# Metaformer layer on one core: the last unit of the scan at 384 tokens, its dense experts as one-hot column blocks, experts 0 and 1 finished in two pieces, four result buffers

## The reference, cut to what matters

```python
x = x + conv_ref(_ln_c(x), ...)          # Mamba block: in_proj, conv, selective scan, out_proj, norm, proj
t = _to_tokens(x)                        # 4 * 1024 tokens of 64 channels
t = t + ffn_ref(_ln_t(t), ...)           # 8 experts, one for each token, capacity 640

def step(h, inp):                        # the scan, over the 1024 tokens of an image, 128 channels, 16 states
    u_t, d_t, B_t, C_t = inp
    dA = jnp.exp(d_t[..., None] * A)
    h = dA * h + (d_t * u_t)[..., None] * B_t[:, None, :]
    y = jnp.einsum('bdn,bn->bd', h, C_t)

logits = x @ gate_w + gate_b             # ffn_ref
idx = jnp.argmax(softmax(logits)); prb = probs[idx]
pos = cumsum(one_hot)[idx] - 1           # rank of the token in its expert
kept = pos < C                           # C = 640
buf = zeros((E, C, D)).at[idx, pos_safe].set(x, mode='drop')
hmid = relu(einsum('ecd,edf->ecf', buf, w1) + b1)   # 64 -> 256
ybuf = einsum('ecf,efd->ecd', hmid, w2) + b2        # 256 -> 64
y_tok = ybuf[idx, pos] * (prb * kept)
```

## Time and profile before

| | us |
|---|---|
| median of 3 runs | 415.32 (412.15 to 419.61) |
| span of the profiled execution, first to last instruction | 398.3 |
| what lies around the span, if the profiled execution was a median one | 17.0 |
| busy: PE, DVE, ACT, POOL | 306.8, 308.8, 235.3, 281.8 |
| granted TensorE clock, mean | 0.880 of full speed |
| moved by DMA | 78.68 MB |

### The profile page before, as it was taken

The page is one execution under the profiler, slowest core; times in us unless marked ns, Lnnn a source line. Parts: engine busy times, 40 slices in busy tenths (PEclk is TensorE's granted clock), DMA queues, the critical chain, the costliest instruction groups (busy, mean ns, idle before and its releaser), DMA issues. The chain is left out here.

```text
span 398.3 us, 4350 instructions
## 1 busy us (share of the span) xinstructions
PE 306.8 (77%) x1257; PEld 180.7 (45%) x1257; DVE 308.8 (78%) x360; ACT 235.3 (59%) x519; POOL 281.8 (71%) x201
## 2 busy tenths in 40 slices
PE   7832978675996988589799769579879569999940
PEld 3311423222644343264434426346458446898940
DVE  4799995999899969878994789999998315667630
ACT  4456696723888595387849774746566135546320
POOL 3435845989696459989973999997688702477771
PEclk9965898989999799889869978999898859999975
DMA  5187999999688935858994366799931073000000
GB/s 102 31 278 258 265 270 343 416 216 381 256 281 285 363 122 183 316 194 275 320 322 166 111 235 208 268 305 365 288 84 31 15 199 79 4 16 18 21 12 0
DMA packets 43986, 78.68 MB, mean 198 GB/s; under 512 B 16050, under 2 KB 26093, under 8 KB 43962
## 3 DMA queue, kind: packets, MB, share of 16 engines
q1 hardware_dynamic: 41066, 73.88, 56.9%
q0 software_dynamic: 2896, 4.53, 4.1%
HBM read 72.30 MB, written 7.54 MB: 200 GB/s over the span
## 5 line engine op out<-in xcount | busy, mean ns | idle before, releaser
L509 POOL TENSOR_TENSOR prod<-h,csb 128x1024 f32<-128x1024 f32 (+1 forms) x64 | 143.9, 2254 | 34.4 <-DVE h L1305 12.4
L973 PE MATMUL Yp<-prod,ident 128*128 128x512 f32 (+1 forms) x256 | 127.6, 630 | 30.5 <-POOL prod L509 30.5
L1305 DVE TENSOR_TENSOR_SCAN h<-dA,Bp 128x1024 f32<-128x1024 f32 (+2 forms) x58 | 119.8, 2065 | 14.4 <-ACT dA L691 10.1
L973 PEld LDWEIGHTS Yp<-prod,ident 128*128 128x128 f32 x256 | 49.7, 207 | 91.5 <-issue 45.4
L1264 DVE TENSOR_TENSOR Bp<-Cp,bsb 128x1024 f32<-128x1024 f32 (+1 forms) x58 | 67.8, 1168 | 6.2 <-DMA bsb<-bc_rows 4.0
L691 ACT ACTIVATE dA<-delta,aneg 128x1024 f32<-128x1024 f32 (+1 forms) x58 | 62.9, 1095 | 12.7 <-DVE h L1305 8.3
L605 POOL DMA_INDIRECT out_dram<-dA,csb x30 | 30.0, 1002 | 28.3 <-DVE dA L1495 20.0
L548 POOL DMA_INDIRECT slots<-rows_,slot x30 | 30.2, 1005 | 6.6 <-issue 4.3
L1140 PE MATMUL Cp<-prod,w1s 128*128 128x384 f32 (+1 forms) x64 | 21.6, 462 | 0.0
L1154 PEld LDWEIGHTS Bp<-w2s,prod 128*128 128x128 f32 x152 | 18.1, 192 | 1.8 <-issue 0.3
L1481 DVE TENSOR_TENSOR dA<-Bp,b2s 128x320 f32<-128x320 f32 (+1 forms) x8 | 3.8, 475 | 19.2 <-PE Bp L1154 19.2
(11 more groups left out here) (289 smaller groups left out, 605.8 us busy)
## 6 DMA issues: line engine op xcount, KB each, us to landing
bsb<-bc_rows SPq DMA_DIRECT2D x48, 512.0 KB, 6.5
csb<-bc_rows SPq DMA_DIRECT2D x48, 512.0 KB, 5.8
bsb<-bc_rows SPq DMA_DIRECT2D x16, 384.0 KB, 5.9
csb<-bc_rows SPq DMA_DIRECT2D x16, 384.0 KB, 6.9
slots<-fill POOLq DMA_DIRECT2D x1, 2600.0 KB, 24.2
csb<-slots SPq DMA_DIRECT2D x6, 325.0 KB, 5.0
bcs<-bc_rows SPq DMA_DIRECT2D x2, 512.0 KB, 12.3
xs_in<-in_x_dram SPq DMA_DIRECT2D x1, 768.0 KB, 5.5
```

The source lines that it names most:

```text
L509: po.tensor_tensor(prod[:, k % 4, c], h[:, k % 3, c], csb[:, k % CSLOTS, c], ALU.mult).then_inc(s_pP, 1)
L973: ins = te_.matmul(Yp[:, c], idn, prod[:, k % 4, c], start=False, stop=(n == 15), skip_group_check=True)
L1305: ins = ve.tensor_tensor_scan(h[:, k % 3, c], decays, drives, h[:, k % 3, c.start - 1:c.start] if i else 0.0, ALU.mult, ALU.add)
```

## The change

`LT` becomes 3: `CARRY` has 5 tiles (640 tokens) and `LAST` has 3 (384 tokens). In `LAST` two states share a buffer instead of four, with 8 pairs of rows for B and 8 for C; the pairs 4 to 7 go to `bsb` and `csb`, after the rows of `CARRY`. The slots are read into other tiles (`fz`, `xnT`, `bcs`), and SP waits for fewer products before it. POOL scatters all tiles of `CARRY` ahead of the products of the pairs 5 to 7. The steps of `back(LAST)` are interleaved with experts 0, 1 and 2 instead of standing ahead of them. The experts' first product contracts over 64 rows, with the odd experts on partitions 64 to 127. Experts 0 and 1 are finished in two pieces each, and `yo` has four buffers.

The dense experts become blocks: DVE lays the normed tokens, times the one-hot choice, into 8 column blocks of 64 (`xm`); PE transposes them two experts at a time (`dense_turn`), `dense_up` sums four products of contraction 128 (two experts each) and one for the bias, and `dense_down` multiplies by the second weights of all 8 experts at once (512 columns), from which DVE picks the chosen expert (`select`). All but `dense_down(2)` stands ahead of the last `down`.

```diff
-HX = C + E
 CHUNKS = [(e, k0, k1) for e in range(E) for k0, k1 in ((0, 3), (3, ET))]
...
+EARLY = 2
+FINISH = CHUNKS[:2 * EARLY] + [(e, 0, ET) for e in range(EARLY, E)]
+OUTS = 4
 R_RES, R_PRB, R_ID, ROW = C, 2 * C, 2 * C + 1, 2 * C + 2
-LT = 2
+LT = 3
...
+            def bring_pair_B(p):
+                if p >= 4:
+                    sp.wait_ge(s_mul, N * LAST - CSLOTS + p - 3)
+                sp.dma_start(rows_B[p], bc_rows[B - 1, 2 * p:2 * p + 2, span(LAST)].unsqueeze(0).broadcast_to([P, 2, LW])
+                             ).then_inc(qb_in[p], 16)
+            def bring_pair_C(p):
+                if p >= 4:
+                    sp.wait_ge(s_pP, N * LAST - CSLOTS + p - 3)
+                sp.dma_start(rows_C[p], bc_rows[B - 1, N + 2 * p:N + 2 * p + 2, span(LAST)].unsqueeze(0).broadcast_to([P, 2, LW])
+                             ).then_inc(qc_in[p], 16)
...
+                    if v == CARRY and n in (4, 6, 9, 12):
+                        bring_pair_B((4, 6, 9, 12).index(n))
+                    if v == CARRY and n in (7, 8, 10, 13):
+                        bring_pair_C((7, 8, 10, 13).index(n))
+            for p in range(4, N // 2):
+                bring_pair_B(p)
+                bring_pair_C(p)
             store_residual(CARRY)
-            sp.wait_ge(s_pP, N * LAST)
-            sp.wait_ge(s_mul, N * LAST)
+            sp.wait_ge(s_pP, N * LAST + 8)
...
             scatter(CARRY - 1, 0, 2)
             products(0)
             scatter(CARRY - 1, 2, 3)
             products(1)
-            scatter(CARRY - 1, 3, 5)
+            scatter(CARRY - 1, 3, 4)
             products(2)
+            scatter(CARRY - 1, 4, 6)
             products(3)
-            scatter(CARRY - 1, 5, 7)
+            scatter(CARRY - 1, 6, 8)
             products(4)
+            scatter(CARRY, 0, UNITS[CARRY][2])
             products(5)
-            scatter(CARRY - 1, 7, 8)
             products(6)
-            scatter(CARRY, 0, 1)
             products(7)
             back(LAST, 13)
-            scatter(CARRY, 1, UNITS[CARRY][2])
...
+            back(LAST, 2)
+            back(LAST, 3)
             channels(0)
             channels(1)
+            hidden(0)
+            back(LAST, 5)
+            channels(2)
+            hidden(1)
+            back(LAST, 8)
+            channels(3)
+            hidden(2)
+            back(LAST, 10)
+            channels(4)
+            hidden(3)
+            back(LAST, 12)
+            channels(5)
+            hidden(4)
             back(LAST, 14)
-            for i in range(len(CHUNKS)):
-                if 2 <= i + 1 < len(CHUNKS):
+            channels(6)
+            hidden(5)
+            for i in range(6, len(CHUNKS)):
+                if i + 1 < len(CHUNKS):
                     channels(i + 1)
                 hidden(i)
...
+                if i == 8:
+                    dense_channels(0)
+                    dense_channels(1)
+                if i == 9:
+                    dense_channels(2)
+                    dense_channels(3)
+                if i == 10:
+                    dense_channels(4)
+                if i == 11:
+                    dense_hidden(0)
+                if i == 12:
+                    dense_hidden(1)
...
-                    te_.matmul(Cp[:, k * HALF:k * HALF + (k1 - k0) * P], w1s[:, e, k * P:(k + 1) * P],
-                               xT[:, e % 2, k0 * P:k1 * P], start=True, stop=True).then_inc(e_up, 1)
+                        pe.wait_ge(b_n2, V)
+                    te_.matmul(Cp[:, k * HALF:k * HALF + (k1 - k0) * P], w1k[half_of(e), e // 2, k * P:(k + 1) * P],
+                               xT[half_of(e), k0 * P:k1 * P], start=True, stop=True).then_inc(e_up, 1)
...
+                if i > 2 * EARLY:
                     pe.wait_ge(e_y, i)
+                elif i >= 2:
+                    pe.wait_ge(e_y, i - 1)
...
+            def dense_turn(p):
+                if p == 0:
+                    pe.wait_ge(b_xm, 1)
+                if p == 1:
+                    pe.wait_ge(e_y, 2 * EARLY)
+                if p >= 2:
+                    pe.wait_ge(d_xT, p - 1)
                 for t in range(LT):
-                    ins = te_.transpose(Yp[0:HX, HALF + t * P:HALF + (t + 1) * P], hx[:, t, :], idn)
+                    if p < E // 2:
+                        ins = te_.transpose(Yp[:, p % 2 * HALF + t * P:p % 2 * HALF + (t + 1) * P],
+                                            xm[:, t, 2 * p:2 * p + 2, :].rearrange("p e c -> p (e c)"), idn)
+                    else:
+                        ins = te_.transpose(Yp[0:E, t * P:(t + 1) * P], ohf[:, t, :], idn)
                 ins.then_inc(d_tr, 1)
...
+            def dense_up(k):
+                dst = Yp[:, k * HALF:k * HALF + LW]
+                pe.wait_ge(d_xT, E // 2 + 1)
+                for p in range(E // 2):
+                    te_.matmul(dst, w1k[:, p, k * P:(k + 1) * P], xkT[:, p, :], start=(p == 0), stop=False)
+                te_.matmul(dst, b1k[:, k * P:(k + 1) * P], ohT, start=False, stop=True).then_inc(d_up, 1)
+            def dense_bias():
+                pe.wait_ge(b_idx, V)
+                for t in range(LT):
+                    ins = te_.matmul(M0[:, t * C:(t + 1) * C], ohT[:, t * P:(t + 1) * P], b2r[:, :], start=True, stop=True)
+                ins.then_inc(d_b2, 1)
+            def dense_down(t):
+                if t < 2:
+                    pe.wait_ge(d_hid, 2)
                 else:
...
+                    pe.wait_ge(d_sel, t - 1)
+                for k in range(2):
+                    ins = te_.matmul(Yp[:, t % 2 * HALF:(t % 2 + 1) * HALF], hid[:, k, t * P:(t + 1) * P], w2s[:, :, k, :],
+                                     start=(k == 0), stop=(k == 1))
                 ins.then_inc(d_dn, 1)
...
             add_state(CARRY, 15)
             back(CARRY, 1)
             add_pair(0)
-            add_pair(1)
             back(CARRY, 4)
             back(CARRY, 5)
             back(CARRY, 6)
+            add_pair(1)
+            for n in range(8, 13):
+                back(CARRY, n)
             add_pair(2)
...
             add_pair(3)
-            add_pair(4)
             back(CARRY, 15)
...
+            for p in range(4, 8):
+                add_pair(p)
+            pe.wait_ge(late_in, 16 * 6)
+            back(LAST, 1)
             turn(0)
-            for i in range(len(CHUNKS)):
+            turn(1)
+            back(LAST, 4)
+            up(0)
+            turn(2)
+            up(1)
+            down(0)
+            back(LAST, 6)
+            turn(3)
+            up(2)
+            down(1)
+            back(LAST, 8)
+            turn(4)
+            up(3)
+            down(2)
+            back(LAST, 10)
+            back(LAST, 12)
+            turn(5)
+            up(4)
+            down(3)
+            turn(6)
+            up(5)
+            back(LAST, 15)
+            for i in range(6, len(CHUNKS)):
                 if i + 1 < len(CHUNKS):
                     turn(i + 1)
-                if i == 1:
-                    down(0)
                 up(i)
...
+                if i % 2 == 0:
+                    down(EARLY + i // 2 - 1)
+                if i == 8:
+                    dense_turn(0)
+                    dense_turn(1)
+                if i == 9:
+                    dense_turn(2)
+                    dense_turn(3)
+                if i == 10:
+                    dense_turn(4)
+                if i == 11:
+                    dense_up(0)
+                if i == 12:
+                    dense_up(1)
+                if i == 13:
+                    dense_down(0)
+                    dense_bias()
+                if i == 14:
+                    dense_down(1)
+            down(len(FINISH) - 1)
+            dense_down(2)
...
+                        ve.tensor_tensor(ohf[:, :, :], work(4, nt), over(bs[:, 21, 0:nt], E), ALU.is_equal).then_inc(b_oh3, 1)
+                        dve.wait_ge(b_oh3, 1)
+                        ve.tensor_tensor(ohr[:, :, :], ohf[:, :, :], over(bs[:, 12, 0:nt], E), ALU.mult).then_inc(b_oh3, 1)
+                        dve.wait_ge(b_oh3, 2)
+                        ve.tensor_tensor(xm, cg[:, 0:nt, :].unsqueeze(2).broadcast_to([P, nt, E, C]),
+                                         ohr[:, :, :].unsqueeze(3).broadcast_to([P, nt, E, C]), ALU.mult).then_inc(b_xm, 1)
...
+            def pair(p):
+                drive_pair(p)
+                scan_last(2 * p)
+                scan_last(2 * p + 1)
+            pair(0)
             back(CARRY, 0)
...
+            pair(1)
             back(CARRY, 3)
...
+            pair(2)
             back(CARRY, 7)
...
+            pair(3)
+            drive_pair(4)
+            scan_last(8)
             back(CARRY, 13)
             back(CARRY, 14)
-            scan_last(13)
+            scan_last(9)
             back(CARRY, 15)
...
+            for p in range(5, 8):
+                pair(p)
...
-                if e >= 2:
-                    dve.wait_ge(e_out[e % 2], 16 * ET * (e // 2))
```

(102 more changed lines are left out.)

224 lines of the change are left out of this document (69 added, 155 removed).

## The result

| | before | changed |
|---|---|---|
| median time, us | 415.32 (412.15 to 421.62, 5 runs) | 438.39 (437.36 to 447.53, 5 runs) |
| profiled execution: time / span / mean granted clock | 400.0, inferred below / 398.3 / 0.88 | 447.53 / 445.8 / 0.795 |
| changed / before | | 1.059 [1.053, 1.065] |

Slower by 5.9% (the medians as they stand differ by 23.1, 5.6%), where 418.6 was forecast. The ratio leaves out executions more than 1.5% above the fastest of their kernel, and the profiled one of the changed kernel, 9 over its median, is such an execution. I read it for order, clock and gaps; a second profile (`e11`, 443.53) has the same gaps to 0.02 for experts 0 to 4, 3.8 earlier.

The account below looks back on a forecast made before the run. DVE was taken to bound the kernel until LAST, then a chain through all engines, then POOL's scatters; the experts' end moving from 391.1 to 394.4 gave +3.3, so 415.3 + 3.3 = 418.6 us, range 409.5 to 424.5.

Parts of the forecast that it names:

- Contraction over 64: Experts' first products on PE: 32 mode changes cost 0.07 each at most, up to 2.2 us; taken as 0.
- The drain of the tiling mode: Experts on PE: switching between 64-row and 128-row products drains TensorE, 0.07 at most per change, 2.2 us for all.
- S = 283.1: Start of LAST's first drive on DVE, 289.08 before; the smaller CARRY brings it 6.0 earlier.
- `turn(0)` at S + 38.3: Start of the experts on PE, 38.3 after LAST's first drive: 321.4, against 324.28 before.
- `turn(0)` to `turn(6)` 19.4: Experts 0 and 1 interleaved with back(LAST): 19.4 us, between 16.1 if handoffs hide and 25.1 if in line.
- rival A: Handoffs between turn(0) and turn(6) hide, 16.1 us: no change at 415 (chance 0.16), or towards a 408 floor (0.06).
- B: Rival: interleaved steps stall in line, 25.1 us from turn(0) to turn(6); +9.0 in all, 424; chance 0.15.
- The dense experts, 5.9 more ahead of the last `down`: Dense blocks cost PE 13.9 against 14.0, but more stands before expert 7's down, which ends 5.9 later after turn(6).
- Edits at nothing: Four result buffers cost nothing; memsets, weight mask and xT filling 0 to 0.3; late DMAs and SP's wait 0 to 0.7.
- Around it lie 17.0: Time outside the profiled span of 398.3, if that execution was a median one; the sum was added to 415.3.
- PE has 4.4 to spare: Kernel before, end of the experts: expert 7 is ready at 380.3, POOL comes to it only at 384.7.
- Rival C: The DMAs take back CARRY's gain: LAST's first drive only 3 earlier, +6.3 in all, 421.5; chance 0.15.

Follow-up runs that it names:

- e11: The changed kernel once more, unedited, for a second profile; 443.53 us.
- e1: The changed kernel with the experts' first product contracting over 128 rows again, the other expert's half filled with zeros; 417.19 us, ratio 1.011.
- e7: The changed kernel with 128 rows in the experts' first product and LAST of 2 tiles instead of 3; 417.67, 418.95, 427.35 and 427.46 us.
- e14: The changed kernel with 128 rows in the experts' first product, run again for a second profile; 413.30 us.
- e8: The changed kernel with 128 rows, and the dense down products of blocks 0 and 1 moved behind expert 7's down; 415.1 us, ratio 1.003.
- e9: As e8, but with dense_turn(4) one chunk earlier; 416.57 us, ratio 1.003.
- e10: As e8, but with two result buffers instead of four; 415.61 us, ratio 1.006.
- e12: The kernel before, unchanged, run again for a profile whose own time is known; 419.04 us.

## Why the prediction was wrong, point by point

- **The step that failed: "Contraction over 64", "I take 0 for my sum".** I priced 64 rows by a change of mode between two shapes and stopped there. All my prices of PE after `turn(0)` were full-clock ones ("at the full clock and with prices from"), and nothing asked whether the edit keeps the clock. It does not: `e1` against the changed kernel, 417.2 and 438.4, makes it 21 us (20 by the two ratios). In the table of stages 20.7 of it lie behind the first scatter. An estimate from the rows gives some 6 of the 21 to the change of shape (12 chunks at 0.50 with 0.43 and 4 at 1.00 with 0.29) and the rest, some 15, to the clock. In the trace before the only products of few rows among the experts were the dense blocks of 72, and even the last eight, in a row, ran at 1.00; it did not show the effect. So a rival with a price of its own was due: all experts at 1.2 GHz, 0.425 for 0.273.
- **The drain of the tiling mode.** The bound was wrong too: "a change costs 0.07 at most and all of them 2.2" was read from logits of 8 columns, and among the experts a chunk's two changes cost 0.29 to 0.43, not 0.14. The Trainium skill, "TensorEngine Tiling (Array Packing)", Key Properties, has a mode change drain TensorE. The trace agrees for 64 rows, and shows nothing of the kind for 72 and 96. The Trainium skill, "TensorE: Matmul & The Clock Gate", What's actually happening, lets the clock depend on how busy TensorE has been. By the profile's busy time the trace differs: PE was busy 5.00 of 5 us at 0.50. The rows in use counted.
- **S = 283.1, `CARRY` -6.0 with 0 to 3 lost.** Right within its bounds. Single profiles give 283.33, 281.74, 287.33; over all, S is 286.4 in nine profiles with `CARRY` of 640 tokens (291.49, 287.33, 283.33, 281.74, 288.22, 286.43, 286.36, 286.20, 286.22) and 290.6 in six of before and its variants (289.08, 295.07, 285.91, 291.37, 291.76, 290.37). So -4.2, give or take about 3. `e7`, with 768 tokens and all else changed, has 285.56, so it is not shown that the tokens make the 4.2.
- **`turn(0)` at S + 38.3.** 39.0 in `e1`, 36.9 in `e14`, and 36.8 to 42.5 over `e8`, `e9` and `e10`. First scatter 10.3 behind it: 10.7 in all five. In the changed kernel 14.4: the clock is already falling.
- **`turn(0)` to `turn(6)` 19.4, between 16.1 and 25.1.** 21.2 in `e1` (322.29 to 343.46), 20.8 in `e14`. A little long, inside the bounds; rival A is out, B falls short of its 25.1. Expert 2 begins on DVE 26.6 after `turn(0)` in `e1`, not 31: that row of mine was too late.
- **The dense experts, 5.9 more ahead of the last `down`.** Forecast for the stage from first scatter to end: 62.7 for 55.9, +6.8. Measured +5.5 (82.4 against 76.9). Both stages are 20 longer than the ones that I worked out, since the execution that I read had no late results and no low clock at its end; that this cancelled in the difference is luck. `e8` takes 3.3 of it back by the order that I named. My 13.9 for the dense blocks on PE were about 1 short: in `e1` a `dense_up` takes 3.57 for my 3.25, a `dense_down` 1.81 for 1.72.
- **Edits at nothing.** Four result buffers: `e10` against `e8`, 0.5, inside the spread. Held.
- **The sum.** -4.2 + 3.0 + 5.5 = +4.3, against my -6.0 + 2.5 + 6.8 = +3.3. `e1` measured +1.1%, 4.7, with an interval of 1 to 8. The terms besides the 64 rows held within what these runs can tell; that their sum came within 1 to 2 us is in part luck, since S alone is known to about 3 and the middle term varied from 1.9 to 7.5.
- **"Around it lie 17.0, if the profiled execution was a median one".** It was not; 1.7 lie around it. The sum was of differences, so this did not move the forecast. But the prices stood on an execution without the late results, and "PE has 4.4 to spare" and "one gap" describe an execution of 400 us, not 415. In `e12` POOL has gaps of 5.83, 7.12 and 3.18.
- **Rival C** may be part of the truth (1.8 of the 6.0 are missing from S, within its spread), without effect on the sign.
